# A second buffer for the exponentials of a state-space convolution, and finer waits in the last normalisation, in an 8-core Trainium2 kernel

## The reference

```python
x = x + LN(attn(LN(x)))        # [2, 8192, 1024]
x = x + LN(ffn(LN(x)))
# attn, the part around the first edit:
A_bar  = clip(exp(-exp(A_log) * dt[:, None]))          # [1024, 16]
B_proj = x_proj @ W_B.T * dt.mean()                    # [.., 16]
A_mean = exp(t[:, None, None] * log(A_bar)).mean(1)    # [L, 16]
x_mean = causal_conv(B_proj, A_mean)                   # over time, one filter per state
y = (x_mean @ W_C.T + D_skip * x_proj) * silu(z)
# ffn: int8-like activations, ternary weights
h   = silu(depthwise_conv3(bit_linear(x, w1)))         # 4096 wide
out = bit_linear(h, w2)                                # 1024 wide; then LN, + x
```

## Time and profile before

| what | value |
|---|---|
| median of the timed runs | 9301.55 us (2 runs, 9301.52 to 9301.58) |
| the profiled execution's own time | 9306.53 us |
| its span on the slowest core, core 6 | 9305.0 us |
| spans of the eight cores | 9247.2 to 9305.0 us |
| mean granted TensorE clock of the cores | 0.609 to 0.611 of full |
| busy time of PE, DVE, ACT, POOL in the span | 2909.8, 3487.4, 860.0, 438.6 us |

### The profile page before, as it was taken

The page is one execution under the profiler, slowest core; times in us unless marked ns, Lnnn a source line. Parts: engine busy times, 40 slices in busy tenths (PEclk is TensorE's granted clock), DMA queues, the critical chain, the costliest instruction groups (busy, mean ns, idle before and its releaser), DMA issues.

```text
span 9305.0 us, 47108 instructions; the slowest of 8 cores (9247.2 to 9305.0 us)
## 1 busy us (share of the span) xinstructions
PE 2909.8 (31%) x12144; PEld 1445.4 (16%) x12144; DVE 3487.4 (37%) x6318; ACT 860.0 (9%) x1765; POOL 438.6 (5%) x452
## 2 busy tenths in 40 slices
PE   3545454112556634444222110101011020103464
PEld 1121312100123333222111100101001010101121
DVE  0111011101121211333344667576675757654212
ACT  0111111111100011000100101101011010110000
POOL 0000000000000000000000011011110102100000
PEclk9955555555577855666555655656566565655686
DMA  1010100111011010111211000000000000021112
GB/s 31 28 42 32 43 27 32 32 30 32 28 38 35 34 37 24 34 32 32 72 51 35 6 12 11 7 15 7 12 6 12 15 8 12 1 108 45 59 40 60
DMA packets 184909, 283.14 MB, mean 30 GB/s; under 512 B 76689, under 2 KB 139371, under 8 KB 180229
## 3 DMA queue, kind: packets, MB, share of 16 engines
q1 hardware_dynamic: 179528, 263.35, 9.2%
q0 software_dynamic: 5120, 16.78, 0.6%
HBM read 223.21 MB, written 55.10 MB: 30 GB/s over the span
## 4 chain that ended last, share of the span: by engine, by line
DVE 35%; PE 28%; DMA 15%; issue 11%; ACT 5%; SPq 2%; DVEq 1%; POOL 1%; ACTq 0%; POOLq 0%
PE ps L240 21%; DVE a_xh L261 7%; PE ps L243 6%; DVE a_xh L257 4%; DMA a_st<-s_logat 3%; DVE a_xh L249 3%; DVE a_w L249 2%; DVE a_st L261 2%; SPq L82 2%; DMA s_wlo<-a_wr 2%; DMA s_rows<-t_tiny 2%; ACT a_st L269 2%; DVE a_xl L249 2%; DVE a_w L246 2%; DVE a_xl L261 2%
## 5 line engine op out<-in xcount | busy, mean ns | idle before, releaser
L261 DVE SCALAR_TENSOR_TENSOR a_xh<-a_xh 128x1024 f32<-128x1024 f32 x512 | 663.9, 1297 | 54.6 <-DVE a_xh L257 1.8
L243 PE MATMUL ps<-c_id,a_xtm 128*128 128x128 f32 (+3 forms) x728 | 274.1, 442 | 759.0 <-DMA s_wlo<-a_wr 320.7
L240 PE MATMUL ps<-a_xh,a_w 128*128 128x512 bf16 (+2 forms) x1664 | 386.3, 396 | 333.6 <-DMA s_xp<-a_st 129.0
L240 PE MATMUL ps<-a_xtm,a_w 128*128 128x258 bf16 x2048 | 289.9, 286 | 618.0 <-DVE a_xtm L261 449.0
L243 PE MATMUL ps<-c_id,a_xh 128*128 128x128 f32 (+1 forms) x536 | 238.7, 445 | 659.4 <-DVE a_xh L249 392.5
L240 PE MATMUL ps<-a_st,c_o1f 128*1 128x256 f32 (+3 forms) x992 | 412.0, 531 | 90.7 <-DMA a_st<-s_x 46.6
L249 DVE TENSOR_TENSOR a_xl<-ps,a_xh 128x256 bf16<-128x256 f32 (+1 forms) x264 | 110.0, 417 | 869.3 <-ACT a_xh L269 869.3
L257 DVE TENSOR_SCALAR a_xh<-a_xh 128x1024 f32<-128x1024 f32 x512 | 394.8, 771 | 55.8 <-DVE a_xh L261 1.4
L243 PE MATMUL ps<-c_id,t_tiny 2*128 2x2 f32 (+6 forms) x54 | 12.3, 231 | 1258.7 <-DMA t_tiny<-s_rows 1256.3
L249 POOL TENSOR_TENSOR a_xh<-a_xl,t_bt 128x256 f32<-128x256 f32 x256 | 298.8, 1196 | 2119.3 <-DMA t_bt<-s_rows 1377.9
L240 PE MATMUL ps<-t_bt,a_st 128*128 128x16 f32 x1024 | 228.3, 374 | 325.4 <-ACT a_st L269 325.4
(11 more groups left out here) (173 smaller groups left out, 4403.6 us busy)
## 6 DMA issues: line engine op xcount, KB each, us to landing
a_st<-s_logat SPq DMA_DIRECT2D x64, 512.0 KB, 4.0
a_xh<-w SPq DMA_DIRECT2D x64, 512.0 KB, 3.9
a_xh<-w SPq DMA_DIRECT2D x16, 2048.0 KB, 8.2
a_xtm<-xp SPq DMA_DIRECT2D x48, 512.0 KB, 4.8
s_hq<-a_big POOLq DMA_DIRECT2D x64, 256.0 KB, 3.2
a_xh<-s_hq SPq DMA_DIRECT2D x128, 128.0 KB, 3.4
a_st<-s_x SPq DMA_DIRECT2D x64, 129.0 KB, 3.2
s_xp<-a_st SPq DMA_DIRECT2D x8, 1025.0 KB, 5.6
```

Of the source, the lines that this page charges most:

```text
L240: e.matmul(o, l, r, start=s1, stop=s2), after=after)
L243: return P.op(T, lambda e, o=out, i=in_, d=ident: e.transpose(o, i, d), after=after)
L261: e.scalar_tensor_tensor(o, x, s, y, op0=p0, op1=p1), after=after)
```

## The change

It has three edits. The first gives the table loop two buffers, `sb_ds` and `sb_m`, in turn: a table waits for the matmul that read its own buffer last (`qlast`), no longer for the matmul recorded last. The matmuls keep their order.

```diff
     xmm = []
+    qlast = [[], []]
     for s_ in range(S):
         for dc in range(KD):
-            qb = act(sb_ds.ap(), sb_i1.ap(), AF.Exp,
-                     scale=sb_la.ap()[:, dc * 16 + s_:dc * 16 + s_ + 1], after=hs + xmm[-1:])
-            xmm.append(mmo(ps[1].ap()[:, s_ * 16:(s_ + 1) * 16],
-                           sb_ds.ap(),
-                           caps(sb_xtm, dc * 16 + s_, [[2176, 128], [128, 16]]),
-                           dc == 0, False, after=[qb]))
+            qi = (s_ * KD + dc) % 2
+            qbuf = sb_ds if qi == 0 else sb_m
+            qb = act(qbuf.ap(), sb_i1.ap(), AF.Exp,
+                     scale=sb_la.ap()[:, dc * 16 + s_:dc * 16 + s_ + 1],
+                     after=hs + qlast[qi])
+            mm = mmo(ps[1].ap()[:, s_ * 16:(s_ + 1) * 16],
+                     qbuf.ap(),
+                     caps(sb_xtm, dc * 16 + s_, [[2176, 128], [128, 16]]),
+                     dc == 0, False, after=[qb] + xmm[-1:])
+            xmm.append(mm)
+            qlast[qi] = [mm]
```

```diff
-            f1 = vtt(ysl, ysl, sb_abc.ap()[:, 0:512], ALU.subtract, after=[bm5] + y5e)
+            f1 = vtt(ysl, ysl, sb_abc.ap()[:, 0:512], ALU.subtract,
+                     after=[bm5, y5e[mo]] + st5[-1:])
...
-                                 after=fin + tps[-2:] + prev_evs[-2:] + outs[-2:-1]))
+                                 after=[fin[mo]] + tps[-2:] + prev_evs[-2:] + outs[-2:-1]))
```

## The result

The changed kernel takes 9218.1 us (median of 11 runs, 9212.3 to 9228.5), beside 9302.7 us for the kernel before in the same runs: a ratio of 0.990, with a 95% interval of 0.988 to 0.992. On another chip, in a later comparison, it was 9197.2 against 9292.0 us, ratio 0.990 (0.988 to 0.991). The forecast was 9216.3 us. The gain of 84.6 us in the first comparison stands against a sum of 85.2.

The account below looks back on a forecast made before the run. The table loop was taken as bound by DMAs until 3435.06, then by the one buffer's hand-over; 79.2 us there plus 6.0 us in the last stage gave 85.2 us, so 9301.55 becomes 9216.3 us, range 9201 to 9232 us.

Parts of the forecast that it names:

- The round: Table loop: activation, matmul, next activation into the same buffer, 1.22 us; with two buffers it serves two tables.
- TensorE's distance behind another matmul: Table loop: a matmul right behind another costs TensorE 0.427 us, read from eight in a row early in the trace.
- the ninth matmul: Table loop, after each state's eight steps: takes 0.427 us of TensorE, pushes the next by 0.06 us; state 4.94 us.
- the hidden gain of the first state: Table loop's start: the first state's own 4.8 us gain is worth nothing, lying under the seven doubling DMAs.
- the early stretch: Trace at 122.54 to 154 us: eight groups of the loop's matmul form, taken as evidence that they did not raise the clock.
- The 6.0 us: Last stage: one transpose instead of eight after the last `f3`, 1.49 us less in each of four blocks.
- The rival that let it rise: Table loop: TensorE's clock rises, round 0.98 us, 14 us more gain, 9202 us; chance 0.06.
- rival 2: Table loop: the two chains still run in step, only the last stage gains, 9295.5 us; chance 0.03.
- A dearer hand-over: Table loop: each hand-over costs more, say 0.10 us a table, 12 us back, 9228 us; chance 0.07.
- The slower case: Gate stage behind the loop: clock stays low, 106 to 207 us lost, 9322 to 9423 us; chance 0.01.
- 14 us around the forecast: Whole kernel: margin for when the clock rises in later stages (5 or 6 us) and the 5 us between profiled and timed runs.
- its 5.0 us for a constant: Whole kernel: the profiled execution lay 5.0 us above the timed median, assumed untouched by the edits.

Follow-up runs that it names:

- the early DMAs: Seven doubling DMAs recorded ahead of the chain of states: against the changed kernel's code 9183.2 us; same move on the kernel before, one buffer, 9267.7 us.
- the kernel with four banks: Changed kernel plus four table buffers, doubling DMAs recorded earlier, four PSUM banks and four output slots at the transposes: 9170.9 against 9317.9 us, ratio 0.983.
- the last experiment: Repeat, on another chip, with four table buffers, doubling DMAs recorded earlier, four PSUM banks and four output slots: 9146.1 against 9292.0 us, ratio 0.984.

## Why the prediction was right

**The table loop.** The mechanism held step by step. The round stayed 1.22 us and served two tables; TensorE's distance behind another matmul was 0.42 us; the ninth matmul pushed the round by 0.06 us; a state took 4.94 us, the predicted number; the first ninth matmul stood where the DMAs put it, 29.06 us in; and the loop took 104.0 us, against 103.8 from the forecast. The experiments show the parts apart: the old wait gives 183 us although there are two buffers, four buffers move the limit to TensorE at the price of the earlier trace rows, and the early DMAs show the hidden gain of the first state as 24.2 against 19.7 us, so 4.5 us, where I had 4.8. One argument on the way was wrong: I called the early stretch (28.53 of 35 us busy) denser than the new loop, and the new loop is the denser one, with 64.35 of 74 us. The conclusion on the clock was right all the same, as shown below.

**The last stage.** The 6.0 us are there, as 1.49 us in each of the four blocks, from the last `f3` to the next load (in the last block, to the end). In the whole time they are too small to be seen alone.

**The clock in the loop.** It reads 0.50 with TensorE 64.35 of 74 us busy, and still 0.50 with 61.59 of 62 us. The rival that let it rise is out for this form of matmul. The Trainium skill ("TensorE: Matmul & The Clock Gate", What's actually happening) says that activity releases the throttle. This trace does not agree for the loop's matmuls, which ran for 62 us without a gap and stayed at 0.50.

**The other rivals.** The experiment with the old wait is the kernel that rival 2 describes, two chains in step, and its loop takes 183 us. The changed loop takes 104. A dearer hand-over would have shown as a period above 1.22 us for a pair; there is none. The slower case, a gate stage that stays at the low clock, did not come: from the first load of that stage to the end of its nine tiles core 6 needed 968.0 us before (3602.35 to 4570.35) and 965.1 us after (3524.07 to 4489.14).

**The scatter and the luck.** I had put 14 us around the forecast for the moments at which the clock rises later. The profiles can be split at the loop's start, at `ev1` and at the first load of the last stage. On core 6 the change took 79.1 us from the loop and 7.1 from the last stage. It added 0.9 us ahead of the loop and 7.4 us between `ev1` and the last stage, though neither stretch has an edit. That makes 78.0 us on the span, which became 9227.0 us where the forecast had 9219.8. The stretch behind `ev1` takes 5047 us (median of the cores) in the kernel before, 5058 in the changed one, and 5052 to 5066 in the other experiments; within one execution the cores differ by up to 33 us in it. The stretch ahead of the loop varies no less, which I had not counted: 3382 to 3409 us by the same medians. That it is the clock's rise that moves them was argued, not shown.

The step from the profiled execution to the median did not hold either. I took its 5.0 us for a constant, and in the changed kernel it was 10.4 us (9228.5 against 9218.1). The span came out 7.2 us longer than forecast and that step 5.4 us larger, and the two nearly cancel: 9218.1 us against 9216.3. So the agreement of sum and medians to 0.6 us in the first comparison is largely luck, as the 94.8 us of the second shows. That the loop gives 79 us is not.

## What to carry to other kernels

Where a timeline shows two engines that are never busy at the same time, read the round (one engine, hand-over, the other, hand-over) and divide it by the number of buffers, down to the busier engine's own distance from start to start; it gave the loop's length to 1 us here for one, two and four buffers. Loosen the wait together with adding the buffer, since the buffer alone gave nothing, and look at what the sped-up loop runs into: here DMAs that waited for more than their data, and took the first 4.5 us. An edit worth 0.06% is judged by the distance between two instructions in the trace, not by the whole time.

## What the runs showed of the hardware that I had not expected

The clock did rise in a place where I thought of no change. In the kernel with four banks, TensorE does 25 float32 transposes in one piece at a block's end, after single ones with idle time between. Windows of core 6 in its last block (span, PE busy, clock, DMA share, GB/s):

```profile
9161.80:9162.80 1.00, 1.00 (x6) 0.50 1.00 418
9162.80:9163.80 1.00, 1.00 (x9) 0.89 0.57 234
9163.80:9164.80 1.00, 0.06 (x1) 1.00 0.82 336
```

The clock goes to the high level 4 us into the piece, and nine transposes stand in that microsecond where six had; core 4 of the last experiment shows the same (0.70 and then 1.00, eight transposes in the microsecond of the rise). It is no single case: in this kernel's profiled execution a rise stands at the end of every one of the 32 blocks (eight cores, four blocks each), 2.8 to 6.0 us after the first of the 25 transposes. In the changed kernel, where the same 25 transposes come one and then three times eight with waits between, it stands at none of the 32. So the clock rose behind these transposes in a row, and not in 62 us of the loop's matmuls.

The Trainium skill ("TensorE: Matmul & The Clock Gate", Part 4: PE-mode transpose) says that the high clock doesn't engage for transposes, which don't count as TensorE being busy in the same way. These rows differ, and they decide for this kernel.

A second point: at the start of an execution the clock column can't be used. It reads 1.00 from the first microsecond, while float32 passes there take 1.01 us, against 0.59 in the gate stage at 1.00. A pair of passes of the same form, just ahead of the rise in the gate stage of the kernel before, shows what it takes at 0.50:

```profile
3640.50:3650.50 10.00, 3.16 (x11) 0.50 0.00 0
3647.34 1.01 PE L240 MATMUL ps<-a_w,c_o1f 128*1 128x256 f32 x2 [9.14 <-DVE a_w L261]
```

So TensorE ran at the low level at 172 us, whatever the column says.
